# The order of the sums and projections on TensorE in the attention passes of a graph network

## The chip, the cores and the metric

One core of a Trainium2 chip runs the whole program. The metric is the device time of one execution in microseconds; the number given for a kernel is the median of its runs. TensorE is called PE (its weight loads PEld), VectorE DVE, ScalarE ACT, GpSimd POOL, SyncE SP.

## The reference

3125 nodes with 64 features, 100000 edges sorted by destination. Two attention layers (8 heads, then 4), then a dense network on neighbour sums, with a residual and a layer norm behind each half. One attention layer is:

```python
xl = (x @ Wl).reshape(N, heads, Dh)
xr = (x @ Wr).reshape(N, heads, Dh)
e = jax.nn.leaky_relu(xl[src] + xr[dst], NEG_SLOPE)
logits = jnp.einsum('ehd,hd->eh', e, att)
m = jax.ops.segment_max(logits, dst, num_segments=n_nodes)
a = jnp.exp(logits - m[dst])
denom = jax.ops.segment_sum(a, dst, num_segments=n_nodes)
alpha = a / denom[dst]
out = jax.ops.segment_sum(alpha[:, :, None] * xl[src], dst, num_segments=n_nodes)
return out.mean(axis=1) + bias
```

## The kernel before

The program runs in stages: a set-up that orders the edges, then for each attention layer a preparation, an edge pass (`edge_pass`, line 866) and a merge of nodes, then the neighbour sums and the dense layers. The change touches the edge pass alone, which runs twice: pass 1 with 8 heads (`C` = 4 projection parts, `HV` = 2), pass 2 with 4 heads (`C` = 2, `HV` = 1).

**Units, quads, chunks.** The edges lie in 900 units of 125 slots; the destinations of a unit lie in one window of 32 nodes. Four units make a quad, five quads (20 units) a chunk; there are 45 chunks (`NCH`). Every engine runs the same two loops, written out when the program is built: over chunks `c`, and in each over `q` = 0 to 4. One turn of the inner loop is called a body here, and "body 3" is the one with q = 3. `lag(c, q, n)` is the quad n bodies back. Since the stages of one quad stand n bodies apart, one body works on several quads at once. The program order on each engine is the order in which the code issues; engines meet at semaphores.

**What PE does in a body** (`body`, line 1083):
- `turn` (lines 994 and 998): the features of a quad's four units, transposed, with the destination's row added; into `ps_x`, from which ACT copies to `xT`.
- `project` (line 1011) for the quad one body back: `C` matmuls of 128 x 500, each into one of two buffers `ps_z`. Part n needs the relu (ACT, line 1127) of the part two before it. An f32 matmul is two instructions in the trace, so the four parts of pass 1 are 8 instructions, a half of them 4.
- `sums` (line 1073) for the quad 15 bodies (three chunks) back, a call for each unit: the weighted features, summed over the slots of the unit for each of the 32 nodes and each head. Two halves of the columns and `HV` groups of heads make 8 instructions a unit in pass 1, 4 in pass 2. The results go to `ps_v`, two buffers of two units each. Before the first unit of a pair, `sums` waits on `chain` until DVE has read the pair that stood in the buffer before (line 1070); behind the second it tells DVE (`v_ready`).
- `reduce` (lines 1023, 1028, 1033) for the quad three back: the logits, into `ps_l`.
- in bodies 0, 1 and 2 also transposes for the chunk two back (lines 1043 to 1061).

The order before is: turn, sums of units 0 and 1, first half of the projections, sums of units 2 and 3, second half, reduce.

**What DVE does in a body** (line 1336): for n = 0 to 3 a `combine` (line 1230, pass 1 and n of 1 to 3 only) for the quad two back and a `run` (lines 1319, 1324) for the quad of the sums. `run` adds a unit's sums to what is carried from the unit before, if both belong to one window:

```python
if u % 2 == 0:
    dve.wait_ge(s["v_ready"], c.val(CU, u + 2))
if c.after(1) or u:
    dve.wait_ge(s["chain"], c.val(CU, u))
```

so the runs form one chain through the whole pass, and run 0 of a body waits for the sums of units 0 and 1 of the same body. Between them stand, in fixed places, the extras: in bodies 0, 1, 2 the weights of five units (`weigh`, line 1302) and small work, in body 3 a scan over 625 columns (`forward`, 1242), four carries (1251) and the weights, in body 4 a scan back (`backward`, 1259), the maxima (1266), the difference (1272) and a copied row (1221).

**What ACT does in a body** (line 1170): it copies logits, the turned features (line 1118) and the rows of the next chunk (line 642, from the gathered tiles), then takes the relus of the projections (line 1127). In body 0, ahead of the rows, it waits until the next chunk's tiles are there.

**Gathers.** POOL fetches 800 tiles of 125 rows in the order of the edges (line 598), 16 to a group, into a ring of four groups. A group is fetched when ACT has copied the last rows out of its place; SP tells ACT when a chunk's tiles are there (`serve`).

Of the kernel before, what the change touches and what calls it, by code (L numbers as in the profile page):

```python
# [22 lines left out]
Q = 4  # L23
# [106 lines left out]
def lag(turn, q, n):  # L130

    return turn.back((n - q + NQ - 1) // NQ), (q - n) % NQ
# [733 lines left out]
def edge_pass(nc, k, lay):  # L866
# [13 lines left out]
    with ExitStack() as ctx:  # L880
# [53 lines left out]
        with nc.Block() as block:  # L934
# [48 lines left out]
            def _(pe):  # L983
                def turn(c, q, blocks):
                    r = c.slot(XR)
                    if q == 0:
                        pe.wait_ge(lay.copied, c.val(1, 1))
                        pe.wait_ge(s["oht_ready"], c.val(1, 1))
                    if c.after(1) or q >= 2:
                        pe.wait_ge(s["xT_ready"], c.val(NQ, q - 1))  # L990
                    ps = ps_x[(c.slot(2) * NQ + q) % 2]
                    for j in range(Q):
                        n = j * NQ + q
                        pe.matmul(ps[:, j * T:(j + 1) * T], xw[:, bass.ds(blocks[n], 128)],  # L994
                                  oht[c.slot(2)][:, n * T:(n + 1) * T], start=True, stop=True)
                    for j in range(Q):
                        n = j * NQ + q
                        ins = pe.transpose(ps[0:D, j * T:(j + 1) * T], xs[r][:, n, 0:D], k.ident[0:T, 0:T])  # L998
                    ins.then_inc(s["x_ready"], 1)

                def window_blocks(c):
                    pe.wait_ge(lay.listed, c.val(1, 1))
                    return listed(pe, lay, c, 0, (NW - 1) * D)

                def project(c, q, part):
                    g = c.slot(XR) * NQ + q
                    if part == 0:
                        pe.wait_ge(s["xT_ready"], c.val(NQ, q + 1))
                    if c.after(1) or C * q + part >= ZR:
                        pe.wait_ge(s["relu_done"], c.val(NQ * C, q * C + part - ZR + 1))  # L1010
                    pe.matmul(ps_z[part % ZR][:, 0:QT], lay.w_abs[:, part * 128:(part + 1) * 128], xT[q][:],  # L1011
                              start=True, stop=True).then_inc(s["z_ready"], 1)

                def reduce(c, q):
                    g = c.slot(XR) * NQ + q
                    if c.after(1) or q:
                        pe.wait_ge(s["logit_copied"], c.val(NQ, q))
                    if lay.norm:
                        pe.wait_ge(s["relu_done"], c.val(NQ * C, (q + 1) * C))
                    else:  # L1020
                        pe.wait_ge(s["combined"], c.val(NQ * (C - 1), (q + 1) * (C - 1)))
                    for j in range(Q):
                        pe.matmul(ps_l[32 * j:32 * j + 32, 0:T], lay.w_lin[:],  # L1023
                                  xT[q][:, j * T:(j + 1) * T], start=True, stop=False)
                    if lay.norm:
                        for part in range(C):
                            for j in range(Q):
                                ins = pe.matmul(ps_l[32 * j:32 * j + 32, 0:T], lay.sign_part[:, part, :],
                                                rl[(C * g + part) % NE][:, j * T:(j + 1) * T], start=False, stop=part == C - 1)
                        ins.then_inc(s["logit_ready"], 1)  # L1030
                        return
                    for j in range(Q):
                        ins = pe.matmul(ps_l[32 * j:32 * j + 32, 0:T], lay.sign_sum[:],
                                        f[g % 3][:, j * T:(j + 1) * T], start=False, stop=True)
                    ins.then_inc(s["logit_ready"], 1)

                def maxima_out(c):

                    if c.after(1):
                        pe.wait_ge(s["left"], c.val(LEFT))  # L1040
                    pe.wait_ge(s["less"], c.val(1, 1))
                    for i in range(4):
                        ins = pe.transpose(ps_t[0:T, i * 128:(i + 1) * 128], mx[c.slot(2)][:, i * T:(i + 1) * T], k.ident[:])
                    ins.then_inc(s["turned"], 1)

                def fifth_out(c):

                    pe.wait_ge(s["left"], c.val(LEFT, 1))
                    pe.wait_ge(s["exp"], c.val(1, 1))
                    pe.wait_ge(s["falls_ready"], c.val(1, 1))  # L1050
                    pe.transpose(ps_t[0:T, 0:128], mx[c.slot(2)][:, 4 * T:SL], k.ident[:])
                    pe.transpose(ps_t[0:T, 128:256], lg[c.slot(3)][:, 4 * T:SL], k.ident[:])
                    for v in range(HV):
                        ins = pe.matmul(ps_t[:, SCALE + v * Q:SCALE + (v + 1) * Q], where[c.slot(2)][:, v * 128:(v + 1) * 128],
                                        falls[c.slot(2)][:], start=True, stop=True)
                    ins.then_inc(s["turned"], 1)

                def weights_out(c):
                    pe.wait_ge(s["left"], c.val(LEFT, 4))
                    for i in range(4):  # L1060
                        ins = pe.transpose(ps_t[0:T, i * 128:(i + 1) * 128], lg[c.slot(3)][:, i * T:(i + 1) * T], k.ident[:])
                    ins.then_inc(s["turned"], 1)

                def sums(c, q, n):
                    u = Q * q + n
                    st = c.slot(XR) * Q + u // NQ
                    if u % NQ == 0:
                        pe.wait_ge(s["p_ready"], c.val(Q, u // NQ + 1))
                    if n % 2 == 0 and (c.after(1) or u >= 4):
                        pe.wait_ge(s["chain"], c.val(CU, u - 2))  # L1070
                    for v in range(HV):
                        for half in range(2):
                            ins = pe.matmul(ps_v[u // 2 % 2][64 * half:64 * half + 64, u % 2 * VX + v * XW:u % 2 * VX + (v + 1) * XW],  # L1073
                                            p[st % 3][:, u % NQ, v, WN // 2 * half:WN // 2 * (half + 1), :].rearrange("e n h -> e (n h)"),
                                            xs[c.slot(XR)][:, u, :], start=True, stop=True)
                    if n % 2:
                        ins.then_inc(s["v_ready"], 2)
# [5 lines left out]
                def body(c, q):  # L1083
                    if c.there():
                        turn(c, q, blocks)
                    zc, zq = lag(c, q, 1)
                    bc, bq = lag(c, q, 15)
                    rc, rq = lag(c, q, 3)
                    for half in range(2):
                        if c.after(3) and bc.there():  # L1090
                            sums(bc, bq, 2 * half)
                            sums(bc, bq, 2 * half + 1)
                        if (c.after(1) or q >= 1) and zc.there():
                            for part in range(C // 2 * half, C // 2 * (half + 1)):
                                project(zc, zq, part)
                    if q == NQ - 1 and c.back(-1).there():
                        blocks[:] = window_blocks(c.back(-1))
                    if (c.after(1) or q >= 3) and rc.there():
                        reduce(rc, rq)
                    b = c.back(2)  # L1100
                    if c.after(2) and b.there():
                        if q == 0:
                            maxima_out(b)
                        if q == 1:
                            fifth_out(b)
                        if q == 2:
                            weights_out(b)
                pe.wait_ge(lay.ld_x, 16)
                blocks[:] = window_blocks(fixed(0))
                chunks(pe, LAST, body)  # L1110

            @block.scalar
# [1083 lines left out]
```

## Time and profile before

| | |
|---|---|
| median of 3 runs | 3819.62 us (3816.06 to 3821.36) |
| the profiled execution | 3812.78 us, span 3811.0 us |
| mean granted clock of TensorE | 0.919 of full speed |
| pass 1, from its first turn to its last run | 197.5 to 1753.3 us |
| pass 2, from its first turn to its last run | 1992.8 to 3242.1 us |

In the page, busy times are given by engine with their share of the span. In a list of groups a row is one line of the code on one engine: busy time, mean of one instruction, idle time of the engine ahead of it and what ended that. In a timeline a row merges instructions of the same kind that follow one another: start, time from the first start to the last end, engine, line, tiles, count, and in brackets the engine's idle time ahead and what released it. The end of a matmul is modelled, and the next starts before it; so the time that PE takes for a piece of work is read here from the start of one row to the start of the next.

### The profile page before, as it was taken

The page shows a single profiled execution, that of the slowest core. Times are in us where ns is not written, and L with a number is a line of the kernel's source. Part 1 is how long each engine was busy: PE and PEld are TensorE (multiplying, and loading weights), DVE is VectorE, ACT ScalarE, POOL GpSimd, SP SyncE. Part 2 cuts the span into 40 slices and gives each one's busy share as a digit, 9 for nine tenths or more (in the row PEclk, how much of TensorE's full clock was granted, in tenths as well). Part 3 has the DMA queues.
Part 4 walks back from the last instruction along what each step waited for, and adds up shares of the span by engine and source line. Part 5 has one row for each costly group of instructions (what it writes and reads, how often), then busy time and mean ns, then how long its engine had stood idle before and what let it go on. Part 6 is the DMA issues. An engine that isn't in the chain of part 4 may idle for free. (4 is left out here: it accounts for less than half of the span.)

```text
span 3811.0 us, 89063 instructions
## 1 busy us (share of the span) xinstructions
PE 3136.0 (82%) x31400; PEld 1856.8 (49%) x31400; DVE 2677.0 (70%) x6673; ACT 1944.4 (51%) x5497; POOL 2500.8 (66%) x1949
## 2 busy tenths in 40 slices
PE   0369999999999999994629799797997978559886
PEld 0235555555555555553515455453554535347663
DVE  3538888888888888886745466464664647489972
ACT  3346556666665666651306455454554544158761
POOL 4488787687687687406378888888888870557620
PEclk9989999999999999996759899898998988579997
DMA  3323333333333333214222233232332322211210
GB/s 62 59 51 75 79 82 82 76 88 83 75 84 80 75 90 82 70 53 100 57 46 63 58 74 75 61 75 60 70 75 61 75 60 44 40 32 38 44 41 22
DMA packets 417512, 249.11 MB, mean 65 GB/s; under 512 B 258173, under 2 KB 380449, under 8 KB 416562
## 3 DMA queue, kind: packets, MB, share of 16 engines
q0 software_dynamic: 97392, 70.80, 10.8%
q10 hardware_dynamic: 237600, 89.88, 9.3%
q1 hardware_dynamic: 82086, 82.74, 8.7%
q8 instruction: 261, 4.28, 0.5%
q14 instruction: 173, 1.42, 0.1%
HBM read 135.21 MB, written 105.95 MB: 63 GB/s over the span
## 5 line engine op out<-in xcount | busy, mean ns | idle before, releaser
L1011 PE MATMUL L_e_ps_z<-L_e_xT,L_w_abs 128*128 128x500 f32 x2700 | 1382.6, 622 | 193.1 <-ACT L_e_rl L1127 192.3
L598 POOL DMA_INDIRECT L_e_tiles<-in_x_dram,src_tile x800 | 1107.9, 1385 | 350.3 <-issue 234.1
L598 POOL DMA_INDIRECT L_e_tiles<-x_d,src_tile x800 | 1010.2, 1263 | 250.2 <-issue 237.7
L1127 ACT ACTIVATE L_e_rl<-L_e_ps_z 128x500 f32<-128x500 f32 x1350 | 778.8, 586 | 573.0 <-PE L_e_ps_z L1011 571.0
L1319 DVE SCALAR_TENSOR_TENSOR L_e_acc<-L_e_acc,L_e_row,L_e_ps_v 128x130 f32<-128x130 f32 (+1 forms) x1440 | 447.4, 311 | 620.2 <-PE L_e_ps_v L1073 434.4
L1011 PEld LDWEIGHTS L_e_ps_z<-L_e_xT,L_w_abs 128*128 128x128 f32 x2700 | 444.7, 191 | 480.1 <-issue 370.1
L642 ACT ACTIVATE L_e_xs<-L_e_tiles 125x64 f32 x1800 | 308.8, 248 | 390.1 <-issue 255.6
L1073 PEld LDWEIGHTS L_e_ps_v<-L_e_xs,L_e_p 125*64 125x64 f32 x8400 | 318.3, 141 | 357.8 <-issue 175.8
L1073 PE MATMUL L_e_ps_v<-L_e_xs,L_e_p 125*64 125x65 f32 x8400 | 425.8, 235 | 19.4 <-DVE L_e_acc L1319 15.5
L1118 ACT ACTIVATE L_e_xT<-L_e_ps_x 128x500 f32<-128x500 f32 x450 | 264.8, 588 | 236.5 <-PE L_e_ps_x L998 236.4
L1230 DVE SCALAR_TENSOR_TENSOR L_e_f<-L_e_rl,L_sign,L_e_f 128x500 f32<-128x500 f32 x450 | 329.1, 731 | 9.9 <-ACT L_e_rl L1127 6.6
L1302 DVE TENSOR_TENSOR L_e_p<-L_e_ohc,L_e_ae 125x640 f32<-125x640 f32 x420 | 333.6, 818 | 0.0
L1794 POOL DMA_INDIRECT g_xs<-x_d,src_idx x168 | 208.5, 1241 | 142.1 <-POOLq L1743 58.6
L1909 ACT ACTIVATE g_cnt<-g_ps_c 125x400 bf16<-125x400 f32 x512 | 257.1, 503 | 65.7 <-PE g_ps_c L1845 56.4
L998 PE MATMUL L_e_ps_x<-ident,L_e_xs 125*64 125x125 f32 x1800 | 268.2, 271 | 0.0
L1939 DVE TENSOR_SCALAR g_ohk<-t_keys_n,t_key_of 125x200 bf16<-125x200 bf16 x1024 | 237.4, 326 | 1.6 <-PE g_ps_c L1845 1.6
L1023 PEld LDWEIGHTS L_e_ps_l<-L_e_xT,L_w_lin 128*32 128x32 f32 x3600 | 71.2, 108 | 335.0 <-issue 334.0
L942 POOL DMA_INDIRECT L_node_max<-L_max_d,max_idx x50 | 62.1, 1243 | 253.8 <-DMA L_max_d<-L_e_me 239.2
L1845 PE MATMUL g_ps_c<-g_ohk,g_ohr 125*128 125x200 bf16 x1024 | 177.0, 256 | 49.2 <-DVE g_ohk L1939 46.1
L994 PE MATMUL L_e_ps_x<-L_e_oht,L_e_xw 96*128 96x125 bf16 x1800 | 176.9, 220 | 36.9 <-DVE L_e_oht L1210 36.9
L1855 PE MATMUL g_ps_s<-g_x,g_cnt 125*128 125x192 bf16 x1600 | 195.7, 248 | 10.3 <-DVE g_sums L1945 10.2
L1023 PE MATMUL L_e_ps_l<-L_e_xT,L_w_lin 128*32 128x125 f32 x3600 | 190.4, 283 | 0.8 <-issue 0.5
(323 smaller groups left out, 4211.0 us busy)
## 6 DMA issues: line engine op xcount, KB each, us to landing
L_v_d<-L_e_acc ACTq DMA_DIRECT2D x225, 260.0 KB
L_e_dlb<-dloc_d SPq DMA_DIRECT2D x90, 468.8 KB, 5.1
L_v_d<-L_e_acc ACTq DMA_DIRECT2D x225, 130.0 KB
L_e_tiles<-in_x_dram,src_tile POOLq DMA_INDIRECT x800
L_e_tiles<-x_d,src_tile POOLq DMA_INDIRECT x800
L_e_lim<-limits_d SPq DMA_DIRECT2D x180, 39.1 KB
L_max_d<-L_e_me SPq DMA_DIRECT2D x45, 78.1 KB
L_e_lim<-limits_d SPq DMA_DIRECT2D x180, 19.5 KB
```

Source lines behind the costliest of these rows:

```text
L598: pool.indirect_dma_start(lay.tiles[:, g % TR * D:(g % TR + 1) * D], None, lay.x_rows, bass.IndirectOffsetOnAxis(k.src_tile[:, g:g + 1], 0 ...
L642: ins = act.activation(lay.xs[c.slot(XR)][:, n, 0:D], lay.tiles[:, bass.ds(places[n], D)], ACT.Copy)
L998: ins = pe.transpose(ps[0:D, j * T:(j + 1) * T], xs[r][:, n, 0:D], k.ident[0:T, 0:T])
L1011: pe.matmul(ps_z[part % ZR][:, 0:QT], lay.w_abs[:, part * 128:(part + 1) * 128], xT[q][:], start=True, stop=True).then_inc(s["z_ready"], 1)
L1023: pe.matmul(ps_l[32 * j:32 * j + 32, 0:T], lay.w_lin[:], xT[q][:, j * T:(j + 1) * T], start=True, stop=False)
L1073: ins = pe.matmul(ps_v[u // 2 % 2][64 * half:64 * half + 64, u % 2 * VX + v * XW:u % 2 * VX + (v + 1) * XW], p[st % 3][:, u % NQ, v, WN // ...
L1118: act.activation(xT[q][:], ps_x[(c.slot(2) * NQ + q) % 2][:, 0:QT], ACT.Copy).then_inc(s["xT_ready"], 1)
L1127: act.activation(rl[n % NE][:], ps_z[part % ZR][:, 0:QT], ACT.Relu, scale=1.0 - SLOPE).then_inc(s["relu_done"], 1)
L1230: dve.scalar_tensor_tensor(out=f[g % 3][:], in0=rl[(C * g + part) % NE][:], scalar=lay.sign[:, part:part + 1], in1=rl[(C * g) % NE][:] if ...
L1302: ins = dve.tensor_tensor(p[n % 3][:, :, v, :, :], ohc[c.slot(2)][:, us, :].unsqueeze(3).to_broadcast([T, NQ, WN, HL]), ae[c.slot(2)][:, u ...
L1319: ins = dve.scalar_tensor_tensor(out=to, in0=prev, scalar=row[c.slot(2)][:, u:u + 1], in1=ps_v[u // 2 % 2][:, u % 2 * VX:(u % 2 + 1) * VX] ...
L1909: act.activation(cnt[i % CR][:, :, 2 * j:2 * j + 2, :], ps_c[n % 2][0:T, 0:2 * KEYS].rearrange("r (u t n) -> r t u n", u=2, n=EN), ACT.Cop ...
```

## The change

The sums leave the place ahead of the first half of the projections. All four calls now stand between the halves: turn, first half of the projections, sums of units 0 to 3, second half, reduce. Everything else, on every engine, is as it was, the waits inside `sums` too.

```diff
                     for half in range(2):
-                        if c.after(3) and bc.there():
-                            sums(bc, bq, 2 * half)
-                            sums(bc, bq, 2 * half + 1)
+                        if half and c.after(3) and bc.there():
+                            for n in range(Q):
+                                sums(bc, bq, n)
                         if (c.after(1) or q >= 1) and zc.there():
                             for part in range(C // 2 * half, C // 2 * (half + 1)):
                                 project(zc, zq, part)
```

## Rows read from the trace of the kernel before

**Rows 1.** The page, busy time of each engine, share of the span, instructions.

```profile
PE 3136.0 (82%) x31400; PEld 1856.8 (49%) x31400; DVE 2677.0 (70%) x6673; ACT 1944.4 (51%) x5497; POOL 2500.8 (66%) x1949
```

**Rows 2.** Two stretches by engine: length, busy us (instructions), granted clock, DMA share, GB/s.

```profile
core 0: us, PE busy (x) PEld busy (x) DVE busy (x) ACT busy (x) POOL busy (x), PEclk, DMA share, GB/s
700.00:900.00 200.00, 198.89 (x1998) 111.34 (x1998) 176.53 (x378) 120.48 (x335) 155.89 (x110) 1.00 0.34 81
2690.00:2890.00 200.00, 188.76 (x2196) 107.94 (x2196) 126.58 (x323) 110.37 (x368) 160.65 (x130) 1.00 0.36 74
```

**Rows 3.** Who waited for whom: PE, 440 to 1690 us (total, times, longest).

```profile
PE L_e_ps_z L1011 <- ACT L_e_rl L1127: 3.1, 5, 0.8
```

**Rows 4.** The same for POOL: 200 to 436, 440 to 1580, 1993 to 3136 us.

```profile
POOL L_e_tiles L598 <- issue: 41.4, 136, 0.3
...
POOL L_e_tiles L598 <- ACT L_e_xs L642: 104.8, 18, 6.5
...
POOL L_e_tiles L598 <- ACT L_e_xs L642: 0.3, 1, 0.3
```

**Rows 5.** Timeline of PE where it waited for a relu.

```profile
436.27 1.10 PE L1011 MATMUL L_e_ps_z<-L_e_xT,L_w_abs 128*128 128x500 f32 x2 [1.83 <-ACT L_e_rl L1127]
...
2716.57 1.08 PE L1011 MATMUL L_e_ps_z<-L_e_xT,L_w_abs 128*128 128x500 f32 x2 [1.47 <-ACT L_e_rl L1127]
...
3139.24 2.00 PE L1011 MATMUL L_e_ps_z<-L_e_xT,L_w_abs 128*128 128x500 f32 x2 [25.62 <-ACT L_e_rl L1127]
```

**Rows 6.** Timeline of PE, pass 1, from body 3 to the next body 0.

```profile
1054.43 0.59 PE L998 MATMUL L_e_ps_x<-ident,L_e_xs 125*64 125x125 f32 x4
1054.95 0.69 PE L1073 MATMUL L_e_ps_v<-L_e_xs,L_e_p 125*64 125x65 f32 x16
1055.57 1.95 PE L1011 MATMUL L_e_ps_z<-L_e_xT,L_w_abs 128*128 128x500 f32 x4
1057.44 0.69 PE L1073 MATMUL L_e_ps_v<-L_e_xs,L_e_p 125*64 125x65 f32 x16
1058.06 1.94 PE L1011 MATMUL L_e_ps_z<-L_e_xT,L_w_abs 128*128 128x500 f32 x4
...
1067.03 0.59 PE L998 MATMUL L_e_ps_x<-ident,L_e_xs 125*64 125x125 f32 x4
...
1070.04 0.69 PE L1073 MATMUL L_e_ps_v<-L_e_xs,x 125*64 125x65 f32 x16
```

**Rows 7.** Timeline of PE, a body at pass 2's start, still without sums.

```profile
2004.83 0.59 PE L998 MATMUL L_e_ps_x<-ident,L_e_xs 125*64 125x125 f32 x4
2005.26 1.84 PE L1011 MATMUL L_e_ps_z<-L_e_xT,L_w_abs 128*128 128x500 f32 x4
2007.04 0.42 PE L1023 MATMUL L_e_ps_l<-L_e_xT,L_w_lin 128*32 128x125 f32 x8
```

**Rows 8.** Timeline of PE, sums split by weight buffer, mid pass 1 and its drain.

```profile
1023.52 0.45 PE L1073 MATMUL L_e_ps_v<-L_e_xs,x 125*64 125x65 f32 x8
1023.80 0.40 PE L1073 MATMUL L_e_ps_v<-L_e_xs,L_e_p 125*64 125x65 f32 x8
...
1713.64 1.57 PE L1073 MATMUL L_e_ps_v<-L_e_xs,x 125*64 125x65 f32 x24
1714.99 0.65 PE L1073 MATMUL L_e_ps_v<-L_e_xs,L_e_p 125*64 125x65 f32 x8
```

**Rows 9.** Timeline of DVE: body 3's run 0, body 4's run 3, two later runs 0.

```profile
1055.74 0.35 DVE L1319 SCALAR_TENSOR_TENSOR L_e_acc<-L_e_acc,L_e_row,L_e_ps_v 128x130 f32<-128x130 f32 x1 [1.33 <-issue]
...
1068.38 0.33 DVE L1319 SCALAR_TENSOR_TENSOR L_e_acc<-L_e_acc,L_e_row,L_e_ps_v 128x130 f32<-128x130 f32 x1
...
1075.17 0.35 DVE L1319 SCALAR_TENSOR_TENSOR L_e_acc<-L_e_acc,L_e_row,L_e_ps_v 128x130 f32<-128x130 f32 x1 [0.58 <-PE L_e_ps_v L1073]
...
1088.97 0.35 DVE L1319 SCALAR_TENSOR_TENSOR L_e_acc<-L_e_acc,L_e_row,L_e_ps_v 128x130 f32<-128x130 f32 x1 [0.99 <-issue]
```

**Rows 10.** Timeline of DVE and PE in pass 1's drain: a run, and sums behind it.

```profile
1716.65 0.32 DVE L1319 SCALAR_TENSOR_TENSOR L_e_acc<-L_e_acc,L_e_row,L_e_ps_v 128x130 f32<-128x130 f32 x1
...
1717.03 0.69 PE L1073 MATMUL L_e_ps_v<-L_e_xs,L_e_p 125*64 125x65 f32 x16 [1.39 <-DVE L_e_acc L1319]
```

## The prediction

> **What bounds the kernel now.** I began with the page: PE is busy 82% of the span, DVE 70%, POOL 66% [rows 1]. That is a mean over two attention passes and what lies around them, so I asked for stretches. In the first pass PE is busy 198.89 of 200 us at the full clock of 2.4 GHz, and DVE 176.53; in the second PE has 188.76, DVE 126.58 and POOL 160.65 [rows 2]. The reader should see two different bounds. In pass 1 PE hardly waits: from 440 us on five times for a late relu, 3.1 us together, and for DVE not at all [rows 3]. Before 436 us POOL's gathers run without a break for ScalarE, after 440 us they wait 18 times for it: early on the gathers lead, later PE does [rows 4]. In pass 2 POOL waited for ScalarE 0.3 us in 1143 us: the gathers set its pace, and PE stands, as at 2716.57 or for 25.62 us at 3139.24 [rows 4, 5]. There a faster PE only waits longer.
>
> So the change is worth something in pass 1, after the gathers have stopped leading, and in what follows pass 2's last gather.
>
> I call the turn T (its line 998 part), the two halves of the projections P01 and P23, the sums S01 and S23, the reduction R; a body is one (c, q), body 3 means q = 3.
>
> **What is removed: changeovers on PE.** One body of pass 1 runs T at 1054.43, S01 at 1054.95, P01 at 1055.57, S23 at 1057.44, P23 at 1058.06 [rows 6]. From T to P23: 0.52 + 0.62 + 1.87 + 0.62 = 3.63 us. The new order T, P01, S01, S23, P23 has two pieces that the first chunks, which have no sums yet, show directly: T to P 0.43 (2004.83 to 2005.26), and four projection instructions right behind a turn, up to R, 1.78 instead of 1.87 [rows 7]. Then come 32 sums. Sixteen with their way out to P are 0.62; the inner sixteen lose both changeovers. Their price: eight sums with the way in took 0.28 (1023.52 to 1023.80), so at most 0.56 for sixteen; 24 in one go took 1.35 us at the half clock (1713.64 to 1714.99), so at least 0.45 at full [rows 8]. I take 0.47, since the inner ones are in mid-stream like the 24. New sum: 0.43 + 1.78 + 0.47 + 0.62 = 3.30. A body gets 0.33 us shorter on PE, a chunk of five 1.65.
>
> At this place the Trainium skill, page TensorEngine Tiling, section Key Properties, says that changing the tiling mode drains the engine. By that rule T, with 64 columns like the sums, would run into S freely and pay before P. The rows say the reverse (0.52 into S, 0.43 into P); I go by the rows, and the rule's outcome is a rival below.
>
> **What is moved: S01, behind two projections.** S01 starts 0.43 + 1.78 = 2.21 us behind T instead of 0.52, so 1.69 later in its body. DVE's run 0 (line 1319) waits for it and starts 0.79 behind it (1054.95 to 1055.74) [rows 6, 9]. Behind run 0 on DVE, in order, stand all of that body's combines, runs and extras. In most bodies DVE then waits again: 0.58 us at 1075.17, 0.99 at 1088.97 [rows 9]; there a start 1.69 later only shifts the pattern. Bodies 3 and 4 are different. They carry the scans: from run 0 of body 3 to the end of run 3 of body 4 is 1055.74 to 1068.38 + 0.33, a string of 12.97 us [rows 9], with no wait in it, while PE's two bodies take 12.60 (1054.43 to 1067.03) [rows 6].
>
> **The wait that is added.** S23 of the next body 0 reuses the buffer that run 3 of body 4 reads (the wait on "chain" in sums). Before, S23 started at 1070.04 [rows 6], 1.33 us after that run's end at 1068.71, and nobody noticed. Now take the same chunk with T of body 3 still at 1054.43. S01 starts at 56.64, run 0 at 57.43, the string ends at 70.40, and 0.06 later (run end 1716.97, sums 1717.03 [rows 10]) S23 may go: 70.46. PE gets there at 1067.03 - 2 x 0.33 + 2.21 + 0.47 = 1069.05. It waits 1.41 us in every chunk, with P23, R and the next turn queued behind it. Nothing on PE can fill it; ScalarE waits for P23, and DVE has its own work.
>
> **The chunk.** S23 of body 0 comes 0.42 us later than before (70.46 against 70.04). From there to the next run 0 of body 3 were 18.93 us (1070.04 to 1088.97); now two shorter bodies and the later S01: 18.93 - 0.66 + 1.69 = 19.96. The period is 70.46 - 57.43 + 19.96 = 32.99 us against 1088.97 - 1055.74 = 33.23. So 0.24 a chunk: 1.65 saved on PE less 1.41 given back. Other waits keep room: between P0 and P23, which needs P0's relu, all four sums now lie instead of two, and in body 0 the 1.41 on top; S01 needs run 1 of the body before, which ends over a microsecond earlier; DVE, 5.5 to 6 us of work in bodies 0 to 2, has caught up by body 3 as its 0.99 us of waiting there shows. The weights p are made by DVE a body or more before the sums that read them. No DMA and no queue of SP or POOL moves.
>
> **The sum.** In chunk 7 PE waits at 436.27 for a relu behind rows that POOL fetched without a pause [rows 4, 5]; what was won before is lost there, and P23 of that body 0 stays at its time. From it to run 0 of body 3: -0.66 + 1.69 = +1.03. Then 37 chunks (7 to 44) at -0.24: -8.9. The five later relu waits (3.1 us [rows 3]) stand in body 0 right behind the new wait and vanish into it: -3.1. The drain behind the last chunk is DVE's string, which only starts earlier. Pass 1: -11.0. Pass 2, behind the last rows at 3139.24: some 14 bodies at 0.33 would be 4.6; the first pays its sums behind the stall, and S01 comes later for the last string; I take -2, between 0 and -5. Total -13 us.
>
> The profiled execution took 3812.78 (span 3811.0), the median of three runs is 3819.62, 6.8 above. -13 gives 3799.8 on that execution, **3806.6** on the median. About 0.2% (7.6 us) is what a measurement of this kernel can tell from no change.
>
> **Bounds.** The inner sums at 0.56 give back 0.18 a chunk (two bodies between S23 and run 0), 6.7 us. A release that takes 0.1 longer, or sums that restart slower behind a wait, cost 3.7 for each 0.1. Both: -3. If the early chunks are not reset by the gathers and pass 2 gives all of its 5: -20. So 3796 to 3822, the upper end taking in the case of no change and a small loss.
>
> **Rivals.**
> *No measurable change* (0.21): the wait is 0.1 to 0.25 longer, by the bounds above; 3812 to 3822. For it: what is left is a difference of two terms six times its size. Against: both terms are read in the same 35 us of one stretch.
> *The whole 1.65 is kept* (0.05). For it: DVE is busy only 88% in pass 1 [rows 2], so on average it has room. That needs S23 of body 0 not to wait. 37 x 1.65 and 5: 64 us, 3756. Against: the string of 12.97 us is work in order, and its start is tied to S01.
> *DVE's string grows* (0.06). The runs of a pair now stand beside the sums that PE writes for the next pair, and the combines beside relus in another phase. From 0.24 us a chunk on (2% of 12.97) the sign turns; at 5% (0.65) it costs 37 x 0.41 = 15, less the relus' 3: about 3831. For it: no row shows a run beside sums in full stream. Against: runs at 1716.65 or 1068.38 take 0.32 to 0.35 wherever they stand.
> *The changeover moves to T and P* (0.04). If T to P01 costs 0.52 and 1.87 as S to P does, a body saves 0.15, S01 comes 1.87 later, the period is 13.03 + 18.93 - 0.30 + 1.87 = 33.53: 0.30 a chunk longer, 11 us, less the relus' 3: about 3828. It is what the rule of TensorEngine Tiling would make of it. Against: the rows with T and P side by side.
> *The clock falls in the new waits* (0.03). Had the P23 and R behind each wait to run at 1.2 GHz, some 2.4 us a chunk: 89 us less the gain, about 3895. The rows speak against it: between 2690 and 2890 PE waits 1.47 us in a body 0 and the granted clock is 1.00 throughout [rows 2, 5]. The Trainium skill, page TensorE: Matmul & The Clock Gate, section on psum-queue depth-cycling, tells of short idles between groups of matmuls that made the clock swing; no run here shows it.
>
> **How the numbers follow.** The forecast (a gain of 8 to 23 us) gets 0.61: the terms are read from rows, but what is left is small against them. With the whole gain, faster is 0.66; same 0.21; slower 0.13. The range 3796 to 3822 leaves out the whole gain and the three slower rivals, 0.18.
>
> **What would show it.** Right: pass 1 chunks at 33.0 us; a line-1073 wait of about 1.4 us on DVE's line 1319 once a chunk, in body 0, some 40 of them, 55 to 60 us; T to P 0.43; thirty-two sums in 1.09; relu waits in pass 1 after 440 us gone; pass 2 of equal length but for its end. Wrong: chunks at 31.6 without that wait (whole gain), the string of bodies 3 and 4 above 13.2, T to P above 0.5, or a granted clock below 1 in pass 1.

## The result and the profile after: pass 1 came as forecast, pass 2 became longer

The changed kernel takes 3887.41 us (median of five runs, 3886.39 to 3887.68) where the kernel before takes 3819.62 (five runs, 3815.65 to 3822.50). The ratio is 1.0178, 95% interval 1.0163 to 1.0193: slower by 68 us, where 13 us of gain were forecast. The profiled execution took 3886.41 us, span 3884.6, against 3812.78 and 3811.0.

The page's line of busy times of the kernel after, to be held against [rows 1]:

```profile
PE 3064.0 (79%) x31400; PEld 1853.3 (48%) x31400; DVE 2675.1 (69%) x6673; ACT 1915.7 (49%) x5497; POOL 2610.0 (67%) x1949
```

The counts of instructions are the same. PE is busy 72.0 us less (3136.0 to 3064.0), the direction that dropped changeovers should bring. The surprise is POOL: the same 1949 instructions, none of which the diff touches, took 109.2 us more. Two stretches of the kernel after (length, busy us and instructions of PE, PEld, DVE, ACT, POOL, granted clock, DMA share, GB/s), to be held against [rows 2]:

```profile
700.00:900.00 200.00, 192.08 (x2022) 110.84 (x2020) 179.47 (x383) 119.93 (x342) 156.57 (x110) 1.00 0.34 82
2690.00:2890.00 200.00, 163.62 (x1892) 95.02 (x1892) 109.39 (x277) 95.11 (x322) 164.04 (x119) 0.90 0.32 66
```

In pass 1 (first line) PE does more instructions in 200 us than before, 2022 against 1998. In pass 2 it does fewer, 1892 against 2196, and so do DVE and ACT. POOL is the one engine that is busier there, 164.04 against 160.65, with fewer instructions, 119 against 130. So look at what POOL does in pass 2. The page's groups of instructions (busy us, mean ns of one, idle time before them), the gathers of pass 2, first the kernel before:

```profile
L598 POOL DMA_INDIRECT L_e_tiles<-x_d,src_tile x800 | 1010.2, 1263 | 250.2 <-issue 237.7
```

and the kernel after:

```profile
L598 POOL DMA_INDIRECT L_e_tiles<-x_d,src_tile x800 | 1096.0, 1370 | 250.1 <-issue 237.0
```

The same 800 gathers take 1370 ns instead of 1263: 85.8 us more. Their idle time is unchanged, so nobody came late for them. The waits of the kernel after say the same (PE from 440 to 1690 us; POOL from 440 to 1580 and from 1993 to 3136), against [rows 3, 4]:

```profile
PE L_e_ps_v L1073 <- DVE L_e_acc L1319: 42.0, 37, 1.1
...
POOL L_e_tiles L598 <- ACT L_e_xs L642: 69.0, 14, 5.7
...
POOL L_e_tiles L598 <- ACT L_e_xs L642: 0.3, 1, 0.3
```

POOL waits for ScalarE 0.3 us in pass 2, as before. The granted clock of 0.90 there goes with longer waits of PE for gathered rows: from 1993 to 3136 us it waits 227.6 us for relus behind them, where it waited 140.0, and behind one such wait of 3.70 us the clock was 0.51 (2758.80 to 2761.00 us), near the lower of its two levels, 1.2 GHz. POOL's own idle time is as before, so what POOL lost is in the gathers themselves. Of POOL's other 23 us, 21.6 are the gathers of pass 1 (1107.9 to 1129.5 us); there POOL waits less for ScalarE (104.8 before, 69.0 after, [rows 4]). The account: 85.8 us more for gathers, some 11 less in pass 1, makes 75; the two spans differ by 73.6.

**Pass 1, one chunk.** Timeline of PE in the kernel after, body 3, the next body 0's turn and its sums, to be held against [rows 6], and DVE's run 0 of body 3, run 3 of body 4, and the next run 0 of body 3, against [rows 9]:

```profile
1048.78 0.59 PE L998 MATMUL L_e_ps_x<-ident,L_e_xs 125*64 125x125 f32 x4
1049.21 1.84 PE L1011 MATMUL L_e_ps_z<-L_e_xT,L_w_abs 128*128 128x500 f32 x4
1050.98 1.15 PE L1073 MATMUL L_e_ps_v<-L_e_xs,L_e_p 125*64 125x65 f32 x32
1052.06 1.94 PE L1011 MATMUL L_e_ps_z<-L_e_xT,L_w_abs 128*128 128x500 f32 x4
...
1060.78 0.59 PE L998 MATMUL L_e_ps_x<-ident,L_e_xs 125*64 125x125 f32 x4
...
1062.98 0.69 PE L1073 MATMUL L_e_ps_v<-L_e_xs,x 125*64 125x65 f32 x16
1064.80 0.69 PE L1073 MATMUL L_e_ps_v<-L_e_xs,x 125*64 125x65 f32 x16 [1.14 <-DVE L_e_acc L1319]
...
1051.77 0.35 DVE L1319 SCALAR_TENSOR_TENSOR L_e_acc<-L_e_acc,L_e_row,L_e_ps_v 128x130 f32<-128x130 f32 x1 [0.99 <-issue]
...
1064.40 0.34 DVE L1319 SCALAR_TENSOR_TENSOR L_e_acc<-L_e_acc,L_e_row,L_e_ps_v 128x130 f32<-128x130 f32 x1
...
1084.73 0.35 DVE L1319 SCALAR_TENSOR_TENSOR L_e_acc<-L_e_acc,L_e_row,L_e_ps_v 128x130 f32<-128x130 f32 x1 [0.64 <-issue]
```

Here every piece is as the prediction has it: T to P 0.43, 32 sums with their way out 1.08 (1050.98 to 1052.06), T to P23 3.28, run 0 0.79 behind its sums, the string 12.97 (1051.77 to 1064.40 + 0.34), S23 released 0.06 after it, and the wait, once a chunk, in body 0. The period is 1084.73 - 1051.77 = 32.96 us; 32.99 was forecast.

**Pass 2, one gather.** Timelines of POOL and DVE, first the kernel before:

```profile
2777.43 1.44 POOL L598 DMA_INDIRECT L_e_tiles<-x_d,src_tile  x1 [0.30 <-issue]
2779.17 1.21 POOL L598 DMA_INDIRECT L_e_tiles<-x_d,src_tile  x1 [0.30 <-issue]
2780.69 1.21 POOL L598 DMA_INDIRECT L_e_tiles<-x_d,src_tile  x1 [0.31 <-issue]
2782.20 1.21 POOL L598 DMA_INDIRECT L_e_tiles<-x_d,src_tile  x1 [0.30 <-issue]
...
2776.40 1.45 DVE L1242 TENSOR_TENSOR_SCAN L_e_fw<-L_e_lim,L_e_lg 128x625 f32<-128x625 f32 x1
...
2780.57 0.28 DVE L1319 SCALAR_TENSOR_TENSOR L_e_acc<-L_e_acc,L_e_row,L_e_ps_v 128x65 f32<-128x65 f32 x1 [0.19 <-PE L_e_ps_v L1073]
2780.77 1.45 DVE L1259 TENSOR_TENSOR_SCAN L_e_mx<-L_e_lim,L_e_fw 128x625 f32<-128x625 f32 x1
```

and the same place of a chunk in the kernel after:

```profile
2772.22 1.46 POOL L598 DMA_INDIRECT L_e_tiles<-x_d,src_tile  x1 [0.30 <-issue]
2773.98 1.21 POOL L598 DMA_INDIRECT L_e_tiles<-x_d,src_tile  x1 [0.30 <-issue]
2775.50 2.26 POOL L598 DMA_INDIRECT L_e_tiles<-x_d,src_tile  x1 [0.30 <-issue]
2778.07 1.63 POOL L598 DMA_INDIRECT L_e_tiles<-x_d,src_tile  x1 [0.31 <-issue]
2780.00 1.60 POOL L598 DMA_INDIRECT L_e_tiles<-x_d,src_tile  x1 [0.30 <-issue]
...
2771.21 1.45 DVE L1242 TENSOR_TENSOR_SCAN L_e_fw<-L_e_lim,L_e_lg 128x625 f32<-128x625 f32 x1
...
2775.10 0.28 DVE L1319 SCALAR_TENSOR_TENSOR L_e_acc<-L_e_acc,L_e_row,L_e_ps_v 128x65 f32<-128x65 f32 x1
2775.29 1.45 DVE L1259 TENSOR_TENSOR_SCAN L_e_mx<-L_e_lim,L_e_fw 128x625 f32<-128x625 f32 x1
...
2777.81 0.80 DVE L1272 TENSOR_TENSOR L_e_lg<-L_e_lg,L_e_mx 128x625 f32<-128x625 f32 x1
...
2779.70 0.82 DVE L1302 TENSOR_TENSOR L_e_p<-L_e_ohc,L_e_ae 125x640 f32<-125x640 f32 x1
```

A gather with nothing beside it takes 1.21 us. Before, the scan of line 1259 began 0.08 us behind a gather's start, and the gather took 1.21 (so did the next one, which began in the scan's last 0.02 us). After, it began 0.21 us ahead of one, and that gather took 2.26: the scan's end at 2776.74, and 1.02 us more. The two gathers behind it began inside a subtraction (line 1272) and a weighing (line 1302) and took 1.63 and 1.60. It is not one bad chunk: between 2200 and 3100 us, each of the 33 scans of line 1259 in the kernel before began 0.06 to 0.09 us behind the start of a gather, which took 1.20 to 1.22 us; each of the 31 in the kernel after began 0.19 to 0.21 us ahead of one, which took 2.27 in the mean.

What fixes that place is the first scan, that of line 1242 in body 3: in both kernels a gather begins inside it and is held. Before, the first scan ends at 2777.85 and the gather under it 1.02 us later; the next gather starts 0.30 behind that, and gathers that nothing holds start 1.51 apart. The second scan begins 2.92 us behind the end of the first, so 2.92 - 1.02 - 0.30 - 1.51 = 0.09 behind a gather's start. After, it begins 2.63 behind (2772.66 to 2775.29), 0.20 ahead of one. The difference of 0.29 comes from PE: its body 3 took 4.37 us from turn to turn (2775.12 to 2779.49) and takes 4.03 (2769.09 to 2773.12), and run 0 of body 4, which waited 0.19 us for its sums, waits no more. In all of those chunks the interval between the two scans is 2.91 to 2.92 us before and 2.63 to 2.64 after, whether PE waited for the chunk's rows not at all or for over 25 us.

PE's fallen clock did not bring this about. The first chunk of pass 2 with sums has the meeting already, a gather from 2051.38 us that took 2.27; PE has no wait between 1990 and 2056 us, and its granted clock is 1.00 from 2005 to 2055. Whether the later waits and the lower clock add meetings elsewhere in a chunk, no run separates.

### The profile page after: what moved, and what is told of

Read it like the earlier page. It is cut to its first block and busy times, and to the rows that moved or that the text cites. A ratio compares the mean times of both kernels' runs of the same rounds, so it can differ in the third digit from the quotient of the medians.

```text
span 3884.6 us, 89063 instructions
## 1 busy us (share of the span) xinstructions
PE 3064.0 (79%) x31400; PEld 1853.3 (48%) x31400; DVE 2675.1 (69%) x6673; ACT 1915.7 (49%) x5497; POOL 2610.0 (67%) x1949
## 5 line engine op out<-in xcount | busy, mean ns | idle before, releaser
L598 POOL DMA_INDIRECT L_e_tiles<-in_x_dram,src_tile x800 | 1129.5, 1412 | 315.8 <-issue 233.8
L598 POOL DMA_INDIRECT L_e_tiles<-x_d,src_tile x800 | 1096.0, 1370 | 250.1 <-issue 237.0
L1011 PEld LDWEIGHTS L_e_ps_z<-L_e_xT,L_w_abs 128*128 128x128 f32 x2700 | 453.4, 195 | 554.2 <-issue 479.7
L1073 PE MATMUL L_e_ps_v<-L_e_xs,L_e_p 125*64 125x65 f32 x8400 | 379.0, 238 | 52.6 <-DVE L_e_acc L1319 48.6
L1909 ACT ACTIVATE g_cnt<-g_ps_c 125x400 bf16<-125x400 f32 x512 | 257.5, 504 | 65.3 <-PE g_ps_c L1845 56.2
```

The costliest lines, as they stand in the source:

```text
L598: pool.indirect_dma_start(lay.tiles[:, g % TR * D:(g % TR + 1) * D], None, lay.x_rows, bass.IndirectOffsetOnAxis(k.src_tile[:, g:g + 1], 0 ...
L1909: act.activation(cnt[i % CR][:, :, 2 * j:2 * j + 2, :], ps_c[n % 2][0:T, 0:2 * KEYS].rearrange("r (u t n) -> r t u n", u=2, n=EN), ACT.Cop ...
```

## The experiments

The theory from these rows: a gather that begins while DVE works on certain instructions is held until that instruction ends; the new order of PE makes a body of pass 2 shorter, which moved DVE's second scan from just behind a gather's start to just ahead of one; since the first scan sets the gathers' place anew in each chunk, each chunk repeats the meeting; and since the gathers pace pass 2, their longer time counts in full. Against it: that PE's order, or pass 1's end, is what costs the time. "Gathers" below are the 800 of pass 2, their total from the page of each run (1010.2 us before, 1096.0 after).

**The new order in pass 1 alone.** In the kernel before:

```diff
-                            sums(bc, bq, 2 * half)
-                            sums(bc, bq, 2 * half + 1)
+                            for n in (range(2 * half, 2 * half + 2) if lay.norm else range(Q * half)):
+                                sums(bc, bq, n)
```

> The new order in pass 1 alone; pass 2 keeps the old order. Theory (the gathers of pass 2 take longer because the scan of line 1259 now begins just ahead of a gather's start instead of just behind it): pass 2 goes back to the length of before, 1249 us from the first turn to the last run, with a gather at 1263 ns in the mean; pass 1 keeps its 11 us; the whole is about 3808, 11 below before. Rival 1 (the scan or the runs of DVE became slower through the new order of pass 1, or the gathers of pass 2 are slow for a reason that does not hang on pass 2's own order, such as where pass 1's end leaves the buffers): pass 2 stays near 1331 and the whole near 3887. Rival 2 (pass 1's gain is paid back between the passes): whole at 3819, no gain.

Measured: 3807.37 us against 3817.14 of the kernel before, ratio 0.9976 (0.9967 to 0.9985), a gain of 9.8 us. Gathers 1012.8 us. From its first turn to its last run, pass 2 lasts 1252.5 us (1249.3 before, 1331.6 after). Pass 1's gain is real and of the size forecast; both rivals fall.

**The new order in pass 2 alone.** The same edit with `not lay.norm`.

> The new order in pass 2 alone; pass 1 keeps the old order. Theory: pass 1 1556 us as before, pass 2 about 1331, chunks of 27.2 us instead of 24.9, gathers at about 1370 ns in the mean; the whole about 3898, some 80 above before. Rival (the slow pass 2 needs the new pass 1): pass 2 at 1249 and the whole at 3820.

Measured (one run): 3892.10, 75 above before. Gathers 1095.6, mean 1370 ns. So the loss is pass 2's own. In the median the two scans are 2.63 us apart in this run, and 2.92 in the run above: that interval hangs on PE's order in pass 2. These two runs do not yet say whether it is PE's order or DVE's scan.

**The scan earlier, PE as before.** In the kernel before, pass 2 only, `backward` (whose scan is line 1259) goes ahead of run 0 of body 4:

```diff
+                        if q == 4 and n == 0 and has1 and lay.norm: backward(one)
                         if add:
                             run(bc, bq, n)
...
-                        if q == 4 and n == 0 and has1:
+                        if q == 4 and n == 0 and has1 and not lay.norm:
                             backward(one)
```

> The kernel before with its PE order untouched; in pass 2 alone the second pair of scans in body 4 is issued on DVE ahead of the body's first run instead of behind it, so that the scan of line 1259 begins some 0.3 to 0.5 us earlier. Theory: the scan now begins ahead of the gather's start, that gather takes 2.26 instead of 1.21 us, a chunk of pass 2 gets 1 to 2.4 us longer, and the whole 40 to 90 above before: 3860 to 3910. Rival (the new order of PE itself costs the time in pass 2): no change, 3815 to 3825.

Measured (one run): 3873.37, 56 above before, with gathers of 1070.8, 60.6 more. Timelines of POOL and DVE in that run:

```profile
2664.35 2.07 POOL L598 DMA_INDIRECT L_e_tiles<-x_d,src_tile  x1 [0.30 <-issue]
...
2663.95 1.45 DVE L1259 TENSOR_TENSOR_SCAN L_e_mx<-L_e_lim,L_e_fw 128x625 f32<-128x625 f32 x1
```

The scan begins 0.40 us ahead of the gather, and the gather takes 2.07. The two reach the same end as above: 1.02 us behind the scan's (2665.40 to 2666.42). PE's order was not touched, so the place of DVE's scan alone is enough for a loss of this size. The sum above gives that place too: the scans are 2.44 us apart here, which puts the second 0.39 ahead of a gather.

**The scan later, by a filler.** In the kernel after, pass 2 only:

```diff
-                            backward(one)
+                            (lay.norm and dve.memset(lay.sq[:, 0:6, :], 0.0)); backward(one)
```

> The changed kernel with one instruction more per chunk of pass 2: a memset of 384 columns of unused scratch on DVE ahead of the second pair of scans in body 4, so that the scan of line 1259 begins some 0.3 us later. Theory: the scan then begins behind the gather's start as it did before the change, the gather that took 2.26 us takes 1.21 again, a group of 16 gathers goes from 27.2 back to some 25 us (25 to 26 if the later work of body 4 now catches another gather), and pass 2 gets 40 to 80 us shorter although DVE does more: 3810 to 3850. Rival (PE's or DVE's order makes the rows come later, DVE is what holds pass 2): 38 chunks each 0 to 0.3 us longer, 3887 to 3900.

Measured (one run): 3892.19, no gain; gathers 1099.7. By the numbers this is the rival's outcome. The timelines show why it is no evidence for it:

```profile
2671.96 2.62 POOL L598 DMA_INDIRECT L_e_tiles<-x_d,src_tile  x1 [0.30 <-issue]
...
2671.88 0.38 DVE L1370 MEMSET L_sq<- 125x384 f32 x1
2672.17 1.40 DVE L1259 TENSOR_TENSOR_SCAN L_e_mx<-L_e_lim,L_e_fw 128x625 f32<-128x625 f32 x1
```

The scan did move behind the gather's start, by 0.21 us, but the filler stood in its old place and was under way when the gather began. The gather took 2.62 and ended 1.01 us behind the scan's end. What differs is the filler under way at its start: of some 1600 gathers of all these traces that have an instruction of DVE with two large inputs in SBUF 0.1 to 0.35 us behind their start, and nothing or only a run under way at it, not one took over 1.23 us. How the hold passed from the filler to the scan, no run shows.

**The scan later, with nothing added.** In the kernel after:

```diff
-                        if q == 4 and n == 0 and has1:
+                        if q == 4 and n == (1 if lay.norm else 0) and has1:
                             backward(one)
```

> The changed kernel; in pass 2 alone the second pair of scans in body 4 is issued on DVE behind the body's run 1 instead of run 0, so that the scan of line 1259 begins some 0.3 us later and no instruction is added. (The memset that should have done this held the gather itself: the gather that met both took 2.62 us.) Theory: the scan begins 0.1 us behind the gather's start instead of 0.2 ahead of it; that gather takes 1.21 instead of 2.26 us; a group of 16 falls from 27.2 to 25 or 26 us; pass 2 40 to 80 us shorter, whole 3805 to 3845. Rival 1 (the later maxima and subtraction now stand closer together and catch the next gathers instead): group at 26.5 or more, whole above 3860. Rival 2 (the order of PE itself costs the time): 3884 to 3892.

Measured: 3834.95 against 3816.41 of the kernel before, ratio 1.0053 (1.0036 to 1.0070), so 18.5 us above before; gathers 1040.9, 55.1 less than after. Timelines of POOL and DVE:

```profile
2692.23 1.21 POOL L598 DMA_INDIRECT L_e_tiles<-x_d,src_tile  x1 [0.30 <-issue]
...
2692.35 1.45 DVE L1259 TENSOR_TENSOR_SCAN L_e_mx<-L_e_lim,L_e_fw 128x625 f32<-128x625 f32 x1
```

The scans are 2.95 us apart, by the sum above 0.12 behind a gather's start. There the gather takes 1.21 again, though PE keeps the new order. One place of one DVE instruction, 0.3 us later, gives back some 55 of the 85.8 us. What stays (30.7 us of gathers, less pass 1's 11, is close to the 18.5) are other meetings: between 2200 and 3100 us, some 70 gathers begin inside a weighing of line 1302, 0.28 us longer in the mean, where the kernel before has 5.

| kernel | gathers of pass 2, us | time, us | less the kernel before beside it |
|---|---|---|---|
| new order in pass 1 | 1012.8 | 3807.37 | -9.8 |
| new order in pass 2 | 1095.6 | 3892.10 | +75.0 |
| before, scan earlier in pass 2 | 1070.8 | 3873.37 | +56.2 |
| after, filler ahead of the scan | 1099.7 | 3892.19 | +75.0 |
| after, scan behind run 1 | 1040.9 | 3834.95 | +18.5 |

**Taking pass 1's wait away.** The wait of 1.14 us a chunk comes from the string's late start: in body 3, S01 stands 1.69 later. So body 3 of pass 1, and pass 2, keep the old order:

```diff
-                            sums(bc, bq, 2 * half)
-                            sums(bc, bq, 2 * half + 1)
+                            for n in (range(2 * half, 2 * half + 2) if (lay.norm or q == 3) else range(Q * half)):
+                                sums(bc, bq, n)
```

> The new order in bodies 0, 1, 2 and 4 of pass 1; body 3 of pass 1 and the whole of pass 2 keep the old order. The long string of DVE (bodies 3 and 4, with the scans) then starts 1.69 us earlier against its turn. Theory: the wait of sums on DVE's run 3 (1.1 us a chunk after the change, 48.8 us in all) is gone, a chunk of pass 1 falls from 32.95 towards 33.23 - 4 x 0.33 = 31.9 us, and where the gathers don't limit it (POOL's waits for ScalarE in pass 1 are down to 66 us with the new order in all five bodies, so at most about that is left) pass 1 gets 30 to 45 us shorter than with the new order in all bodies; whole 3765 to 3785. Rival 1 (DVE's work per chunk is the bound, not where its string starts): chunk at 32.9, whole near 3807, as with the new order in all of pass 1. Rival 2 (the gathers already limit pass 1): PE's waits change from DVE's runs to relus and the whole stays within 10 us of 3807.

Measured: 3779.61 against 3816.41, ratio 0.9907 (0.9890 to 0.9923): 36.8 us faster than before, 27 better than the new order in all of pass 1. The 42.0 us of waits for DVE's runs between 440 us and the pass's end are gone from that list. Both rivals fall, but the chunk is 32.21 us, not 31.9. Timeline of PE (body 3's T and S01, then body 0's sums and the P23 behind) and of DVE (run 0 of body 3, run 3 of body 4):

```profile
1068.62 0.59 PE L998 MATMUL L_e_ps_x<-ident,L_e_xs 125*64 125x125 f32 x4
1069.14 0.69 PE L1073 MATMUL L_e_ps_v<-L_e_xs,L_e_p 125*64 125x65 f32 x16
...
1083.08 1.52 PE L1073 MATMUL L_e_ps_v<-L_e_xs,L_e_p 125*64 125x65 f32 x32
1084.53 1.94 PE L1011 MATMUL L_e_ps_z<-L_e_xT,L_w_abs 128*128 128x500 f32 x4
...
1070.90 0.34 DVE L1319 SCALAR_TENSOR_TENSOR L_e_acc<-L_e_acc,L_e_row,L_e_ps_v 128x130 f32<-128x130 f32 x1
...
1083.52 0.34 DVE L1319 SCALAR_TENSOR_TENSOR L_e_acc<-L_e_acc,L_e_row,L_e_ps_v 128x130 f32<-128x130 f32 x1
```

The 32 sums of body 0 take 1.45 to P23 instead of 1.08. S23 still waits, by 0.37, and the view of waits does not list it since it lies inside a group of sums: read the start of what follows, not only the waits. Run 0 of body 3 came 1.76 behind its sums, not 0.79, as DVE was late from body 2.

**One DVE step out of body 2.** To that kernel, in pass 1, the comparison of line 1214 (0.82 us) goes one body earlier:

```diff
                         if q == 1 and n == 3 and c.back(-1).there():
                             spread_hot(c.back(-1))
+                        if q == 1 and n == 3 and has2 and not lay.norm:
+                            sum_hot(two)
...
-                            sum_hot(two)
+                            if lay.norm: sum_hot(two)
```

> The kernel with the old order in body 3 of pass 1 and in pass 2, and one step of DVE moved besides: in pass 1 the 0.82 us comparison of line 1214 goes from the end of body 2 to the end of body 1. There a chunk still took 32.21 us instead of 31.87, since run 0 of body 3 came 1.76 us behind its sums (DVE was late from body 2), and the last sums of the next body 0 were held up by some 0.35 us. Theory: body 3's run 0 then starts 0.8 to 1.1 us behind its sums, that hold goes, a chunk falls to 31.9 and the whole by another 8 to 14 us, to 3766 to 3772. Rival 1 (the gathers limit pass 1 by now): 3774 to 3782, with PE's waits for relus up by what the chunks lost. Rival 2 (moving a step of DVE changes which gathers it holds): anywhere between, told by the mean of a pass-1 gather.

Measured: 3773.05 against 3812.14, ratio 0.9892 (0.9875 to 0.9908). The interval overlaps the one above, so no further gain is shown, and the chunk is still 32.22. PE's waits for relus are 2.3 us from 440 to 1650 us in both kernels, so the gathers are not what keeps it there. Run 0 of body 3 did come earlier, but the 0.37 stayed. Timeline of PE (body 4's T and sums; body 0's sums and the P23 behind) and of DVE (body 4's runs 0 and 3):

```profile
1072.55 0.59 PE L998 MATMUL L_e_ps_x<-ident,L_e_xs 125*64 125x125 f32 x4
...
1074.75 1.15 PE L1073 MATMUL L_e_ps_v<-L_e_xs,x 125*64 125x65 f32 x32
...
1080.71 1.51 PE L1073 MATMUL L_e_ps_v<-L_e_xs,L_e_p 125*64 125x65 f32 x32
1082.15 1.94 PE L1011 MATMUL L_e_ps_z<-L_e_xT,L_w_abs 128*128 128x500 f32 x4
...
1075.54 0.35 DVE L1319 SCALAR_TENSOR_TENSOR L_e_acc<-L_e_acc,L_e_row,L_e_ps_v 128x130 f32<-128x130 f32 x1 [0.84 <-issue]
...
1081.13 0.34 DVE L1319 SCALAR_TENSOR_TENSOR L_e_acc<-L_e_acc,L_e_row,L_e_ps_v 128x130 f32<-128x130 f32 x1
```

DVE now waits 0.84 ahead of body 4's run 0, which stands 0.79 behind that body's late sums. From there to run 3's end are 5.93 us, so from body 4's S01 to the release of S23 0.79 + 5.93 + 0.06 = 6.78, while PE needs 5.96 for the body and 0.47 for S01. The 0.35 between them is body 4's own. My expectation had named body 3 as the cause, and that was the wrong place. Of the versions that beat both kernels, the one without this move is the smaller edit.

## Why the prediction was wrong: the gathers' price was taken as fixed

The steps for pass 1 held. The changeovers came out at 3.28 for 3.30, the string and the release to the hundredth, the chunk at 32.96 for 32.99. The relu waits of [rows 3] are gone. The last run of pass 1 ends at 1744.21 instead of 1753.32 while the first turn came 2.33 later, 11.4 us in all for 11.0, and the kernel with pass 1's change alone gained 9.8. Only the wait's own size was off, 1.14 for 1.41. PE's 16 sums ahead of it are counted to their end, 0.68 behind their start (1062.98 to 1063.66, the start of the wait), where I had used the 0.47 at which the next would start; that moves time between two names and not the period. Two slips of the working change nothing: in pass 2 PE's wait for a relu stands in body 1, not in body 0 (2716.57), and the bound worked out as -20 is 3799.6, not 3796.

The step that failed is the one on pass 2: "the gathers set its pace, and PE stands", "There a faster PE only waits longer", "No DMA and no queue of SP or POOL moves", and in the sum "Pass 2, behind the last rows at 3139.24 ... I take -2, between 0 and -5". That the gathers set the pace was right, and it made pass 2 the place where every microsecond of a gather counts in full. But the working took a gather for a constant, as if nothing that DVE does could reach it, and asked only who waits for PE. The mean of 1263 ns in the kernel before stands above the 1.21 of most gathers. That difference, 52 ns times 800 or some 42 us, was in the trace to be asked about: some gathers already took longer, and the DVE rows beside them say which, those under the first scan among them. Since the first scan holds a gather in every chunk, what DVE does next stands at the same place against the gathers in every chunk, and a PE body that is 0.3 us shorter shifts it for all chunks at once. Before, the second scan began 0.08 us behind a gather's start; 0.29 earlier it stood ahead of one: +1.05 us for that gather. Sorted by what DVE had under way at a gather's start, the second scan accounts for 40 of the 85.8 us and the weighings for 35.

Counted over 2200 to 3100 us in both traces, gathers that begin inside DVE instructions with two large inputs in SBUF (the scans, the subtraction, the weighing) are held, unless they begin in the last 0.2 us or so; those that begin inside the runs of lines 1319 and 1324, whose other large input is in PSUM, take 1.21 us but for a few that the comparison of line 1210 behind the run catches. That comparison does not fit the pattern: it has one large input, gathers that begin inside it are held too, and of 129 gathers in all traces that it follows by up to 0.35 us, 124 took over 1.25 us. The Trainium skill, page SBUF — State Buffer, states the rule for two inputs: a DVE instruction with two SBUF inputs contends with a GpSimd instruction that reads SBUF (section Who interferes with whom), and whichever of them starts first has the pair of ports for its whole instruction (section SBUF: two separate sides). The rows agree where DVE is first (2.26, 2.07 us). The first of these sections also reports that `tensor_tensor` did not stall a DMA, with a reason that it calls inferred; the gathers held by lines 1272 and 1302 (1.63, 1.60 us) went the other way here. For pass 2's gathers, the rule would have given the rival that was missing: DVE's instructions move against POOL's. From the rows of before, a gather that meets the scan can lose up to the scan's 1.45 us, and one meeting in each of the 45 chunks makes that up to some 65 us.

None of the five rivals was the one. The fallen clock (0.90 in pass 2) looks like the last of them, which was for pass 1; there the clock stayed at 1.00 (700 to 900 us) with a wait of 1.14 us in every chunk. In pass 2 it follows from the gathers: the first meeting came at a granted clock of 1.00, POOL waits for ScalarE no longer than before, and the kernel with the scan behind run 1 gave 55 us of gathers back at the same mean clock (0.907 against 0.906).

## What to carry to other kernels

An engine that sets the pace is not a constant: ask what makes one of its instructions longer than the shortest of its kind, and whether the change moves that. Where a pipeline is locked to such an engine, a shift of a few tenths of a microsecond elsewhere can repeat in every chunk; compare the starts of the two engines' instructions in the trace before, and treat a margin of 0.1 us as a risk with a price. And a reordering that is good in one stage may be made in that stage alone: with the new order in four of five bodies of pass 1 and nowhere else, this kernel is 36.8 us faster.

## What the runs showed of the hardware

- Between the gathers and the scan the hold goes one way here. A scan that begins 0.08 or 0.12 us behind a gather's start takes 1.45 us, the same as one that begins ahead of it, and the gather takes 1.21. The Trainium skill, page SBUF — State Buffer, section SBUF: two separate sides, has the later of the two block fully in either order; for DVE as the later one the rows do not show it.
- A held gather does not resume where it stood: it takes 1.01 to 1.02 us from the scan's end (1.08 from the subtraction's), most of its 1.21, whether the scan's end came 1.05 us behind its start, 1.24, or 1.61 (the runs with the scan earlier, after, and with the filler).
- A hold also sets when the next gathers start. The sum 1.02 + 0.30 + 1.51 from the first scan's end gives the second scan's place against the gathers to 0.01 us in the median, before, after, and with that scan moved earlier or later.
- A gather that began while a memset of 384 columns into SBUF was under way, 0.38 us long and without any input, was held to the end of the scan behind it: 2.62 us, in 28 of 28 cases between 2200 and 3100 us. That a memset alone holds one, no run shows.
